# A three-stage kernel on one core: late states and their statistics in the head of the scan stage, and another order on VectorE in steps 7 to 11

## The chip, the core and the metric

The kernel runs on one core of a Trainium2 chip. The metric is the device time of one execution in microseconds. Times of single instructions come from one profiled execution of the program.

## What is computed

Input is a tensor of 4 batches, 1024 tokens and 256 channels, fp32. Three blocks with residuals follow each other: a coupled feed-forward, a selective scan (Mamba), and the same feed-forward again.

```python
x = x + 0.5 * ffn(layernorm(x))
x = x + mamba(layernorm(x))
x = x + 0.5 * ffn(layernorm(x))

def ffn(x):                       # 3 cycles over all tokens
    gf = global_net(x.mean(axis=1, keepdims=True))
    out = x
    for _ in range(3):
        tf = coupling_net(out)    # 256 -> 256 -> 128 -> 64 -> 1: gelu, gelu, gelu, sigmoid
        c = 0.1 + adaptive_range * (0.7 * gf + 0.3 * tf - 0.5) * 2.0
        out = out + c * twist(out)            # twist swaps and negates quarters of the channels
    return out

def mamba(resid):                 # 512 inner channels, 16 states, 4 taps
    xn = rmsnorm(resid) * norm_w
    skip, x = xn @ skip_w.T, xn @ in_w.T
    x = silu(conv4(x) + conv_b)
    delta = softplus(x @ wd1.T @ wd2.T + wd2_b)
    B, C, A = x @ wB.T, x @ wC.T, -exp(A_log)
    h[t] = exp(delta[t] * A) * h[t-1] + delta[t] * x[t] * B[t]     # per channel and state
    y[t] = sum_n h[t] * C[t] + W_D * x[t]
    return resid + (y * silu(skip)) @ out_w.T
```

## The kernel before

Three programs run one after the other, with a barrier between them: `ffn` ("f1"), `mamba`, and `ffn` ("f2"). The residual `x_tok` stays in SBUF as 32 tiles of 128 tokens by 256 channels, eight for each batch. Every engine runs a list of instructions in order; semaphores alone tie the lists together.

**The feed-forward.** There are 12 steps, one for each batch and cycle, in the order of `ORDER`: batches 0 and 1 alternate through their three cycles (steps 0 to 5), then batches 2 and 3 (steps 6 to 11). A step is a ring: gelu on ScalarE (L529), matmul (L412), gelu (L535), matmul (L424), gelu (L542), matmul (L435), tanh (L561), and on VectorE `update` (L245, L258, L260), whose result the same batch's next step reads two steps later. Since twist is linear, the kernel keeps the two products `a` and `b` of the first weight matrix instead of the state; `turn_by` (L268) and `turn_off` (L277) turn `b` after a batch's first cycle. `update` of a batch's second cycle reads the turned `b`, and the tanh of the second cycle overwrites the coupling that `turn_by` reads (`act.wait_ge(part_ready, ...)` in `tanh4`). The state after three cycles is a combination of the normalised input `z_tok` and its twist with coefficients per token. `coefficients` computes them (14 instructions on 8 elements, L289 to L311), `add_straight` (L319) or, for batches 2 and 3, `finish` on ScalarE (L569) adds the straight part, and `add_across` (L331, L333) the twisted one, 16 instructions for a batch. `measure` (L340, L344) then takes mean and variance of the new `x_tok` for the next normalisation. VectorE's order around the change is its loop over `s`: for s = 7, `coefficients(1)`, `add_straight(1)`, `update(6)`, `add_across(1)`, `turn_by(6)`, `turn_off(6)`; for s = 8, `coupling_base(3)`, `update(7)`, `turn_by(7)`; for s = 9, `update(8)`, `turn_off(7)`; then `update(9)` and, in f1, the two `measure`.

**The scan.** Eight segments of 512 tokens, each of 32 units K: 16 states times two pairs of channel tiles. Per unit, ScalarE writes the decays exp(delta A) into one of two PSUM banks (`decay`, L916), GpSimd the input term `u` into a ring of four (`drive`, L1030), VectorE runs two scans of 512 (L1113), and either VectorE (L1125) or, for 6 states of 16, GpSimd (`weigh`, L1042) multiplies with C. TensorE adds up. Between the units stands the preparation of the next segment by the places in `AT` and `PLACES`: turned tiles (L952), `acc` (L972), the taps of the convolution on VectorE (`convolve`, L1148, with the three columns kept for the next segment in `spill`, L1155 to L1164), silu (L977), projections, softplus over 2048 elements (L988), `take_in` on GpSimd (L1051, two products of delta and x). Segment 0 is prepared before the first scan, with nothing beside it. Ahead of that stand mean and deviation of all 32 tiles in one chain between ScalarE (L894, L896) and VectorE (L1083 to L1096).

## Time and profile before

| | |
|---|---|
| median of 3 runs | 1346.56 us (1346.34 to 1346.61) |
| profiled execution | 1345.62 us, span 1343.8 us |
| VectorE (DVE) | 87% of the span busy |
| GpSimd (POOL) | 65% |
| ScalarE (ACT) | 58% |
| TensorE (PE) | 79%, mean granted clock 0.943 |
| f1, up to its last instruction | 0 to 207.3 us |
| scan stage | 207.6 to about 1158 us |
| f2 | about 1158 us to the end |

Busy shares are means over the whole span, while the stages have different limits. In the rows, f_ stands for a tile of a feed-forward, m_ for one of the scan stage; a line "x8" joins eight like instructions in a row, from the start of the first to the end of the last, which overlap a little. A bracket tells how long the engine stood idle ahead of the instruction and whose end released it.

### The profile page before, as it was taken

How to read it: one execution, taken by the hardware profiler on the slowest of the kernel's cores; microseconds unless marked ns; L12 is line 12 of the kernel's file. 1: busy time of each engine (PE TensorE's matmuls, PEld its weight loads, DVE VectorE, ACT ScalarE, POOL GpSimd, SP SyncE). 2: the span in 40 equal slices, each digit the busy share in tenths (PEclk: the TensorE clock that was granted, in tenths of full speed). 3: DMA queues.
4: the chain of work that ended last, by engine and by line, in shares of the span. 5: the costliest groups of instructions: out<-in, count | busy, mean ns of one | idle time of the engine just before them, and what ended most of it. 6: DMA issues, size and time to landing. Idle time of an engine off the chain costs nothing. (4 is left out here: it accounts for less than half of the span.)

```text
span 1343.8 us, 10915 instructions
## 1 busy us (share of the span) xinstructions
PE 1065.7 (79%) x2688; PEld 459.1 (34%) x2688; DVE 1171.8 (87%) x1764; ACT 774.9 (58%) x1315; POOL 871.6 (65%) x390
## 2 busy tenths in 40 slices
PE   3999644679779889878888988987897867799964
PEld 2434212233233334324334333432432422444411
DVE  3755985599999999999999999999999999576595
ACT  2656465767645656745656674565674434266555
POOL 0000000899989999998999999899999999000000
PEclk9999887889998899999989999999998888899987
DMA  6000000544444444354353443445445443000003
GB/s 204 1 1 1 1 1 2 165 139 151 158 129 162 149 157 156 123 174 144 128 187 116 169 147 139 154 125 188 137 147 170 144 156 109 0 1 1 1 0 126
DMA packets 48000, 146.56 MB, mean 109 GB/s; under 512 B 5504, under 2 KB 14336, under 8 KB 47936
## 3 DMA queue, kind: packets, MB, share of 16 engines
q1 hardware_dynamic: 47440, 145.03, 32.6%
q10 hardware_dynamic: 496, 0.82, 0.2%
q8 instruction: 22, 0.36, 0.1%
q14 instruction: 42, 0.34, 0.1%
HBM read 141.05 MB, written 4.72 MB: 108 GB/s over the span
## 5 line engine op out<-in xcount | busy, mean ns | idle before, releaser
L1030 POOL TENSOR_TENSOR m_u<-m_dx,m_brow 128x1024 f32<-128x1024 f32 x256 | 599.4, 2380 | 1.0 <-DVE m_a_bank L1113 0.9
L916 ACT ACTIVATE m_a_bank<-m_delta,m_negA 128x512 f32<-128x512 f32 x512 | 335.0, 683 | 172.9 <-DVE m_hc L1125 133.4
L1259 PE MATMUL m_y_bank<-m_hc,ident 128*128 128x512 f32 x640 | 327.8, 638 | 102.3 <-DVE m_hc L1125 102.2
L1042 POOL TENSOR_TENSOR m_hc_pool<-m_hid,m_crow 128x1024 f32<-128x1024 f32 x96 | 228.5, 2380 | 28.7 <-DVE m_hid L1113 28.4
L1259 PEld LDWEIGHTS m_y_bank<-m_hc,ident 128*128 128x128 f32 x640 | 119.0, 199 | 289.6 <-DVE m_hc L1125 169.8
L1125 DVE TENSOR_TENSOR m_hc<-m_a_bank,m_crow 128x512 f32<-128x512 f32 x320 | 203.2, 678 | 0.0
L1113 DVE TENSOR_TENSOR_SCAN m_a_bank<-m_a_bank,m_carry,m_u 128x512 f32<-128x512 f32 x160 | 196.5, 1276 | 1.1 <-ACT m_a_bank L916 0.8
L1051 POOL TENSOR_TENSOR m_dx<-m_delta,m_x 128x1024 f32<-128x1024 f32 x16 | 38.1, 2385 | 240.1 <-ACT m_delta L988 240.1
L1259 PE MATMUL m_y_bank<-m_hc_pool,ident 128*128 128x512 f32 x384 | 187.8, 613 | 7.1 <-POOL m_hc_pool L1042 7.1
L1113 DVE TENSOR_TENSOR_SCAN m_a_bank<-m_a_bank,m_u 128x512 f32<-128x512 f32 x160 | 186.7, 1213 | 7.0 <-ACT m_a_bank L916 3.5
L1113 DVE TENSOR_TENSOR_SCAN m_hid<-m_a_bank,m_u 128x512 f32<-128x512 f32 x96 | 111.9, 1208 | 19.4 <-ACT m_a_bank L916 19.1
L1222 PE MATMUL m_w_bank<-m_xn,w 128*128 128x512 f32 x240 | 115.1, 608 | 3.7 <-DVE m_dx L1148 2.6
L1113 DVE TENSOR_TENSOR_SCAN m_hid<-m_a_bank,m_carry,m_u 128x512 f32<-128x512 f32 x96 | 117.8, 1270 | 0.0
L1259 PEld LDWEIGHTS m_y_bank<-m_hc_pool,ident 128*128 128x128 f32 x384 | 75.0, 198 | 105.7 <-issue 87.9
L412 PE MATMUL f_pair<-f_h,w 128*128 128x512 f32 x192 | 94.7, 624 | 6.1 <-ACT f_h L529 6.1
L928 ACT ACTIVATE m_carry<-m_a_bank 128x2 f32<-128x2 f32 x80 | 13.5, 169 | 109.5 <-DVE m_hc L1125 109.4
L529 ACT ACTIVATE f_h<-f_a,w 128x512 f32<-128x512 f32 x96 | 63.6, 713 | 10.8 <-DVE f_a L260 10.8
L1247 PE MATMUL m_y_bank<-m_x,m_diag_d 128*128 128x512 f32 x64 | 43.2, 811 | 33.4 <-DVE m_gate L1135 33.4
L1222 PEld LDWEIGHTS m_w_bank<-m_xn,w 128*128 128x128 f32 x240 | 45.8, 194 | 65.5 <-issue 53.9
L1236 PE MATMUL m_w_bank<-w,m_gate 128*128 128x256 f32 x256 | 59.1, 384 | 9.6 <-DVE m_dx L1148 8.1
L461 PE MATMUL f_pair<-f_z,w 128*128 128x512 f32 x128 | 65.4, 592 | 0.0
L1148 DVE SCALAR_TENSOR_TENSOR m_dx<-m_w_bank,m_conv,m_dx 128x511 f32<-128x511 f32 (+2 forms) x84 | 62.3, 741 | 1.1
(135 smaller groups left out, 1232.4 us busy)
## 6 DMA issues: line engine op xcount, KB each, us to landing
m_brow<-bc_rows SPq DMA_DIRECT2D x128, 512.0 KB, 4.9
m_crow<-bc_rows SPq DMA_DIRECT2D x128, 512.0 KB, 4.0
x_tok<-x_in SPq DMA_DIRECT2D x4, 1024.0 KB, 8.8
out<-x_tok SPq DMA_DIRECT2D x3, 1024.0 KB, 6.4
w<-w_in SPq DMA_DIRECT2D x1, 1024.0 KB, 12.4
out<-x_tok SPq DMA_DIRECT2D x4, 256.0 KB, 2.1
w<-w_in SPq DMA_DIRECT2D x1, 750.0 KB, 10.4
w<-w_in ACTq DMA_DIRECT2D x1, 512.0 KB, 6.0
```

The lines of the kernel that those rows point to most:

```text
L412: last = nc.tensor.matmul(pair[2][:, h, :], w(w256, W256, "w2", k), h1[:, k, half(h)], start=k == 0, stop=k == KD - 1)
L461: last = nc.tensor.matmul(out[:, m, :], second, z[:, b % 2, 1, half(n)], start=False, stop=True)
L529: nc.scalar.activation(h1[:, m, half(h)], source, ACT.Gelu, bias=w128[:, o:o + 1]).then_inc(h1_ready, 1)
L916: nc.scalar.activation(a_bank[K % 2][:, j, :], delta[:, i % 2, c, :], ACT.Exp, scale=negA[:, c, n:n + 1]).then_inc(S["a"], 1)
L1030: nc.gpsimd.tensor_tensor(u[:, K % U_RING, :, :], dx[:, i % 2, 2 * q:2 * q + 2, :], brow[:, K // 2 % ROW_RING, K % 2, :].unsqueeze(1).to_b ...
L1042: nc.gpsimd.tensor_tensor(hc_pool[:, before % POOL_RING, :, :], hid[:, before % POOL_RING, :, :], crow[:, K // 2 % ROW_RING, K % 2, :].uns ...
L1113: nc.vector.tensor_tensor_scan(hid[:, pool_before(K) % POOL_RING, j, :] if by_pool(K) else a, a, u[:, K % U_RING, j, :], 0.0 if i % 2 == 0 ...
L1125: nc.vector.tensor_tensor(hc[:, before % HC_RING, j, :], a_bank[K % 2][:, j, :], crow[:, K // 2 % ROW_RING, K % 2, :], ALU.mult).then_inc( ...
L1148: nc.vector.scalar_tensor_tensor(a[:, s:], b[:, 0:BANK - s], conv[:, c, k:k + 1], a[:, s:], ALU.mult, ALU.add)\
L1222: op = nc.tensor.matmul(b, w256[:, part, o:o + P], xn[:, (p if kind == "in" else i) % 2, part, :], start=part == 0, stop=part == KD - 1)
L1236: op = nc.tensor.matmul(b[:, part * DIM:(part + 1) * DIM], gate[:, d, at:at + P], col("out", d, DIM), start=d == 0, stop=d == KE - 1)
L1259: op = nc.tensor.matmul(y_bank[:, j, :], ident[:, :], source[:, before % ring, j, :], start=False, stop=K % PASS == PASS - 1)
```

## The change

The last states of batches 2 and 3 are no longer added and measured in f1. f1 leaves behind their coefficients (`coef`) and their normalised input (`late`, memory that the scan stage uses as its ring `u`), and the scan stage takes this over. The straight part of batch 2 goes from ScalarE to VectorE (`late_straight` there). Square roots and norms are taken in two halves: tiles 0 to 15 at once, 16 to 31 within segment 0 (`deviation` at units 4 and 8 on ScalarE, `norms` after units 5 and 10 on VectorE). ScalarE's instructions ahead of the first scan are written out in one list, `prologue`; the turned tiles of segment 1 are made there too, the standardising of `x_tok` for segments 0 and 1 comes in units 1, 3, 6 and 7. Softplus is split into two halves in all segments, and in segment 0 the second `take_in` of GpSimd moves to unit 3. VectorE keeps the spill columns of segment 0 after all taps, then adds and measures the late batches. In `ffn`, `coefficients` no longer contains the shifts that only batches 2 and 3 need, and the order of steps 7 to 11 is another, in f1 and f2 alike.

```diff
+def late_tile(mem, at):
+    return mem["late"][:, :, :, :].rearrange("p a b (c d) -> p (a b c) d", d=DIM)[:, at - 2 * BT, :]
...
-        z_tok = sb("z_tok", [P, TILES, DIM])
+        z_tok = sb("z_tok", [P, 2 * BT, DIM])
...
-                nc.vector.tensor_tensor(at(3), at(7), rstd[:, ts], ALU.mult).then_inc(coef_ready, 1)
-                dve.wait_ge(coef_ready, 2 * b + 1)
+                nc.vector.tensor_scalar(at(9), at(5), -0.5, None, ALU.mult).then_inc(coef_ready, 1)
+                dve.wait_ge(coef_ready, b + 1)
+            def shifts(b):
+                ts, n = slice(b * BT, (b + 1) * BT), b - len(ALONE) + 1
+                at = lambda j: coef[:, b % 2, j, :]
+                nc.vector.tensor_tensor(at(3), at(7), rstd[:, ts], ALU.mult).then_inc(shift_part, 1)
+                dve.wait_ge(shift_part, n)
                 nc.vector.tensor_scalar(at(10), at(3), 1.0, None, ALU.add)
                 nc.vector.scalar_tensor_tensor(at(11), at(3), -1.0, moments[:, ts, 0], ALU.mult, ALU.mult)\
-                    .then_inc(coef_ready, 1)
-                dve.wait_ge(coef_ready, 2 * b + 2)
+                    .then_inc(shift_ready, 1)
...
-                if s in (6, 7):
-                    add_across(s - 6)
-                if cycle(s - 1) == 0:
+                if s == 6:
+                    add_across(0)
+                if s == 8:
+                    turn_off(6)
+                if s in (1, 2, 7):
                     turn_by(s - 1)
-                    if s < 8:
-                        turn_off(s - 1)
+                if s in (1, 2):
+                    turn_off(s - 1)
                 if s == 9:
+                    turn_by(7)
                     turn_off(7)
                 if s == 2:
                     sum_up(2)
                 if s == 5:
                     coupling_base(2)
                     sum_up(3)
-                if s in (10, 11) and measure_next:
-                    measure(s - 10)
+                if s == 10:
+                    add_across(1)
+                if s == 11 and leave_late:
+                    measure(0)
+                    measure(1)
             coefficients(2)
-            add_across(2)
+            shifts(2)
+            if not leave_late:
+                add_across(2)
             coefficients(3)
-            if measure_next:
-                measure(2)
-            add_across(3)
-            if measure_next:
-                measure(3)
+            shifts(3)
+            if not leave_late:
+                add_across(3)
...
+            def norms(h, part):
+                ts = slice(h * (TILES // 2), (h + 1) * (TILES // 2))
+                root, square = roots[:, h, 0, :], roots[:, h, 1, :]
+                if part == 0:
+                    dve.wait_ge(S["root"], 2 * h + 1)
+                    nc.vector.reciprocal(rstd[:, ts], root).then_inc(S["rstd"], 1)
+                    dve.wait_ge(S["rstd"], 6 * h + 1)
+                    nc.vector.tensor_tensor(square, rstd[:, ts], rstd[:, ts], ALU.mult).then_inc(S["square"], 1)
+                    dve.wait_ge(S["square"], 2 * h + 1)
+                    nc.vector.tensor_tensor(square, square, moments[:, ts, 1], ALU.mult).then_inc(S["square"], 1)
+                    return
+                dve.wait_ge(S["root"], 2 * h + 2)
+                nc.vector.reciprocal(rrms[:, ts], root).then_inc(S["rstd"], 1)
+                dve.wait_ge(S["rstd"], 6 * h + 2)
+                nc.vector.scalar_tensor_tensor(shift[:, ts], moments[:, ts, 0], -1.0, rstd[:, ts], ALU.mult, ALU.mult)\
+                    .then_inc(S["rstd"], 1)
+                nc.vector.tensor_tensor(scale_n[:, ts], rstd[:, ts], rrms[:, ts], ALU.mult).then_inc(S["rstd"], 1)
+                nc.vector.tensor_scalar(scale_z[:, ts], rstd[:, ts], 1.0, None, ALU.add).then_inc(S["rstd"], 1)
+                dve.wait_ge(S["rstd"], 6 * h + 5)
+                nc.vector.tensor_tensor(shift_n[:, ts], shift[:, ts], rrms[:, ts], ALU.mult).then_inc(S["rstd"], 1)
+            def late_straight():
+                b = BATCH - 2
+                for t in range(BT):
+                    at = b * BT + t
+                    op = nc.vector.scalar_tensor_tensor(x_tok[:, at, :], late_tile(mem, at), coef[:, b % 2, 7, t:t + 1],
+                                                        x_tok[:, at, :], ALU.mult, ALU.add)
+                op.then_inc(S["late_by_dve"], 1)
+                dve.wait_ge(S["late_by_dve"], 1)
+            def late_across(b):
+                for t in range(BT):
+                    at, z = b * BT + t, late_tile(mem, b * BT + t)
+                    if b == BATCH - 1:
+                        dve.wait_ge(S["late_straight"], t + 1)
+                    nc.vector.scalar_tensor_tensor(x_tok[:, at, :P], z[:, P:], coef[:, b % 2, 8, t:t + 1],
+                                                   x_tok[:, at, :P], ALU.mult, ALU.add).then_inc(S["late_added"], 1)
+                    nc.vector.scalar_tensor_tensor(x_tok[:, at, P:], z[:, :P], coef[:, b % 2, 9, t:t + 1],
+                                                   x_tok[:, at, P:], ALU.mult, ALU.add).then_inc(S["late_added"], 1)
+            def late_measure():
+                first = (BATCH - 2) * BT
+                dve.wait_ge(S["late_added"], 4 * BT)
+                for t in range(2 * BT):
+                    op = nc.vector.bn_stats(late_stats[:, t, :], x_tok[:, first + t, :])
+                op.then_inc(S["late_stats"], 1)
+                dve.wait_ge(S["late_stats"], 1)
+                for t in range(2 * BT):
+                    op = nc.vector.bn_aggr(moments[:, first + t, :], late_stats[:, t, :])
+                op.then_inc(S["moments"], 1)
+            norms(0, 0)
+            norms(0, 1)
+            late_straight()
+            late_across(2)
...
+            def softplus(i, g):
+                p, cs = i + 1, slice(2 * g, 2 * g + 2)
+                act.wait_ge(S["step"], p * KE + 2 * g + 2)
+                nc.scalar.activation(delta[:, p % 2, cs], delta[:, p % 2, cs], ACT.Softplus).then_inc(S["delta"], 1)
...
+            def prologue():
+                act.wait_ge(S["rstd"], 6)
+                standardise(0, 0, xn_tok, scale_n, shift_n, "xn_tok")
+                standardise(0, 1, xn_tok, scale_n, shift_n, "xn_tok")
+                late_straight(range(4))
+                take_turned(-2, 0)
+                take_turned(-2, 1)
+                standardise(1, 0, xn_tok, scale_n, shift_n, "xn_tok")
+                standardise(1, 1, xn_tok, scale_n, shift_n, "xn_tok")
+                table_of(ACT.Silu)
+                accumulate(-1, 0)
+                late_straight(range(4, 6))
+                accumulate(-1, 1)
+                late_straight(range(6, 8))
+                accumulate(-1, 2)
+                accumulate(-1, 3)
+                silu(-1, 0)
+                silu(-1, 1)
+                take_turned(-1, 0)
+                silu(-1, 2)
+                take_turned(-1, 1)
+                silu(-1, 3)
+                project(-1)
+                table_of(ACT.Softplus)
+                step_size(-1, 0)
+                step_size(-1, 1)
+                softplus(-1, 0)
+                step_size(-1, 2)
+                step_size(-1, 3)
+                softplus(-1, 1)
+                rates()
...
+                for g, t in enumerate((1, 3, 6, 7)):
+                    if K == t:
+                        standardise(g // 2, g % 2, None, scale_z, shift, "z")
+                for n, t in ((2, 4), (3, 8)):
+                    if K == t:
+                        deviation(n)
...
+                if K == 0:
+                    pool.wait_ge(S["late_added"], 4 * BT)
...
+                    if (i, g) != (-1, 1):
+                        take_in(i + 1, g)
+                if K == 3:
+                    take_in(0, 1)
...
+                if K == AT["conv"][-1] - UNITS:
+                    for c in range(KE):
+                        keep_spill(-1, c, 1)
+                        keep_spill(-1, c, 2)
+                    late_across(BATCH - 1)
+                    late_measure()
+                if K in (5, 10):
+                    norms(1, K // 10)
```

## Rows read from the trace of the kernel before

**Rows 1.** The page, busy time of each engine, its share of the span and its instructions.

```profile
PE 1065.7 (79%) x2688; PEld 459.1 (34%) x2688; DVE 1171.8 (87%) x1764; ACT 774.9 (58%) x1315; POOL 871.6 (65%) x390
```

**Rows 2.** Windows, scan segment 0: window, length, busy us (instructions) per engine, PEclk, DMA.

```profile
250.00:363.00 113.00, 90.28 (x192) 35.42 (x191) 111.26 (x126) 74.83 (x147) 108.64 (x48) 0.95 0.45 150
```

**Rows 3.** Timeline, VectorE and ScalarE, steps 7 to 11: start, us, engine, line; idle before.

```profile
146.46 0.34 DVE L331 SCALAR_TENSOR_TENSOR x_tok<-f_z_tok,f_coef,x_tok 128x128 f32<-128x128 f32 x1
...
150.66 2.35 DVE L268 TENSOR_TENSOR f_part<-f_a,f_cpl 128x1024 f32<-128x1024 f32 x2
...
155.63 0.55 DVE L245 TENSOR_SCALAR f_cpl<-f_cpl,f_slope,f_base 128x512 f32<-128x512 f32 x1
...
161.59 2.35 DVE L268 TENSOR_TENSOR f_part<-f_a,f_cpl 128x1024 f32<-128x1024 f32 x2
...
148.10 1.26 ACT L561 ACTIVATE f_cpl<-f_pair,f_half_b 128x512 f32<-128x512 f32 x2 [1.21 <-PE f_pair L435]
...
158.73 1.33 ACT L529 ACTIVATE f_h<-f_a,w 128x512 f32<-128x512 f32 x2 [5.39 <-DVE f_a L260]
...
171.56 1.27 ACT L561 ACTIVATE f_cpl<-f_pair,f_half_b 128x512 f32<-128x512 f32 x2 [1.21 <-PE f_pair L435]
...
179.88 1.25 ACT L561 ACTIVATE f_stack<-f_pair,f_half_b 32x512 f32<-32x512 f32 x2 [1.21 <-PE f_pair L435]
...
1287.98 1.26 ACT L561 ACTIVATE f_cpl<-f_pair,f_half_b 128x512 f32<-128x512 f32 x2 [1.21 <-PE f_pair L435]
...
1311.52 1.27 ACT L561 ACTIVATE f_cpl<-f_pair,f_half_b 128x512 f32<-128x512 f32 x2 [1.21 <-PE f_pair L435]
```

**Rows 4.** Timeline, VectorE and TensorE at the end of the first feed-forward stage.

```profile
178.24 2.70 DVE L340 BATCH_NORM_STATS2 f_stats<-x_tok 128x6 f32<-128x256 f32 x8
...
185.04 0.24 DVE L289 COPY f_coef<-f_pair 128x8 f32<-128x8 f32 x2
...
186.92 0.16 DVE L311 SCALAR_TENSOR_TENSOR f_coef<-f_coef,moments 128x8 f32<-128x8 f32 x1
...
189.54 1.03 PE L468 MATMUL f_pair<-ident,f_stack 34*128 34x34 f32 x8 [1.38 <-issue]
...
206.66 0.64 DVE L344 BATCH_NORM_AGGREGATE moments<-f_stats 128x2 f32<-128x6 f32 x8
```

**Rows 5.** Timeline, all engines, head of the scan stage before its first scan.

```profile
209.23 0.35 DVE L1083 RECIPROCAL m_rstd<-m_tmp_u 128x32 f32<-128x32 f32 x1 [0.66 <-ACT m_tmp_u L894]
...
211.23 0.19 DVE L1096 TENSOR_TENSOR m_shift_n<-m_shift,m_rrms 128x32 f32<-128x32 f32 x1
...
212.28 2.08 ACT L938 ACTIVATE m_tmp_u<-x_tok,m_shift_n,m_scale_n 128x256 f32<-128x256 f32 x4
...
220.26 0.78 ACT L972 ACTIVATE m_dx<-m_a_bank,m_conv 128x512 f32<-128x512 f32 x1 [1.91 <-PE m_a_bank L1222]
...
229.35 0.27 DVE L1155 TENSOR_SCALAR m_spill<-m_a_bank,m_conv 128x3 f32<-128x3 f32 x1
...
230.57 0.74 DVE L1148 SCALAR_TENSOR_TENSOR m_dx<-m_a_bank,m_conv,m_dx 128x509 f32<-128x509 f32 x1
...
239.60 1.91 ACT L988 ACTIVATE m_delta<-m_delta 128x2048 f32<-128x2048 f32 x1
...
246.20 9.29 POOL L1030 TENSOR_TENSOR m_u<-m_dx,m_brow 128x1024 f32<-128x1024 f32 x4
...
249.65 2.34 DVE L1113 TENSOR_TENSOR_SCAN m_hid<-m_a_bank,m_u 128x512 f32<-128x512 f32 x2 [18.34 <-ACT m_a_bank L916]
```

**Rows 6.** Timeline, all engines, early units of scan segment 0.

```profile
257.56 2.29 DVE L1148 SCALAR_TENSOR_TENSOR m_dx<-m_w_bank,m_conv,m_dx 128x511 f32<-128x511 f32 x3
...
278.44 1.28 ACT L977 ACT_TABLE_LOAD   x1
...
283.39 1.30 ACT L916 ACTIVATE m_a_bank<-m_delta,m_negA 128x512 f32<-128x512 f32 x2
...
284.62 2.34 DVE L1113 TENSOR_TENSOR_SCAN m_a_bank<-m_a_bank,m_u 128x512 f32<-128x512 f32 x2
```

More of the change, by code:

```diff
@@ L631, in _ @@
             tanh4(STEPS - 1, 1)
-            finish(2)
-            finish(3)
+            if not leave_late:
+                finish(2)
+                finish(3)
         @block.sync
@@ L728, in mamba @@
     }
+    EARLY_TURN = ((4,), (5,))
     AT = {
@@ L786, in mamba @@
         here = [(at, kind, c, part) for kind in PLACES if exists(i, kind)
-                for c, ats in enumerate(PLACES[kind]) for part, at in enumerate(ats)]
+                for c, ats in enumerate(EARLY_TURN if (i, kind) == (-1, "turn") else PLACES[kind])
+                for part, at in enumerate(ats)]
         order = list(PLACES)
@@ L833, in mamba @@
         crow = sb("crow", [P, ROW_RING, 2, BANK])
-        u = sb("u", [P, U_RING, 2, BANK])
+        u = mem["late"]
+        expA = sb("expA", [P, KE, STATE])
+        roots = sb("roots", [P, 2, 2, TILES // 2])
         hid = sb("hid", [P, POOL_RING, 2, BANK])
@@ new lines, in take_turned, with accumulate @@
+            def take_turned(i, c):
+                b = work_there((i, "turn", c))
+                for d in range(KD):
+                    o = W128["norm"][0] + d
+                    op = nc.scalar.activation(xn[:, i % 2, d, c * 2 * P:(c + 1) * 2 * P],
+                                              b[:, d * 2 * P:(d + 1) * 2 * P], ACT.Copy, scale=w128[:, o:o + 1])
+                op.then_inc(S["xn"], 1)
+            def accumulate(i, c):
+                p = i + 1
+                ph = p % 2
+                b = work_there((i, "in", c))
+                if c == 0 and i > 0:
+                    act.wait_ge(S["u"], i * UNITS)
+                lo = 0
+                if ph == 1:
+                    lo = TAPS - 1
+                    act.wait_ge(S["spill"], p // 2 * KE + c + 1)
+                    for j in range(lo):
+                        nc.scalar.activation(acc[:, ph, c, j:j + 1], b[:, j:j + 1], ACT.Identity,
+                                             scale=conv[:, c, TAPS - 1:TAPS], bias=spill[:, c, j:j + 1])
+                nc.scalar.activation(acc[:, ph, c, lo:], b[:, lo:], ACT.Identity,
+                                     scale=conv[:, c, TAPS - 1:TAPS], bias=conv[:, c, TAPS:TAPS + 1])\
+                    .then_inc(S["acc"], 1)
@@ new lines, in silu, with project @@
+            def silu(i, c):
+                p = i + 1
+                act.wait_ge(S["conv"], p * KE + c + 1)
+                nc.scalar.activation(x[:, p % 2, c, :], acc[:, p % 2, c, :], ACT.Silu).then_inc(S["x"], 1)
+            def project(i):
+                p = i + 1
+                b = work_there((i, "xproj", 0))
+                if p > 0:
+                    act.wait_ge(S["bc_stored"], 16 * p)
+                nc.scalar.activation(proj[:, :], b[0:XROWS, :], ACT.Copy).then_inc(S["proj"], 1)
@@ L944, in turn @@
                 for g in due(k, "xn_tok"):
[L945 to L946 removed]
+                    if g == 0 and p == SEGS // 2:
+                        act.wait_ge(S["rstd"], 12)
                     standardise(p, g, xn_tok, scale_n, shift_n, "xn_tok")
                 for c in due(k, "xn"):
[L949 to L954 removed]
+                    take_turned(i, c)
                 for g in due(k, "z"):
@@ L1001, in take_out @@
                 nc.scalar.activation(th[:, c, :], b, ACT.Copy).then_inc(S["out_there"], 1)
-            for K in range(-2 * UNITS, TOTAL + UNITS):
+            prologue()
+            for K in range(TOTAL + UNITS):
                 i, k = K // UNITS, K % UNITS
@@ L1287, in build @@
             "moments": sb("moments", [P, TILES, 2]),
+            "late": sb("late", [P, 4, 2, BANK]),
+            "coef": sb("coef", [P, 2, 12, BT]),
         }
```

170 lines of the change are left out of this document (77 added, 93 removed).

## The prediction

> **What bounds the kernel now.** I read the page first. VectorE is busy 1171.8 of 1343.8 us [rows 1], but that is a mean over three stages, so I went to the windows. In one segment of the scan VectorE works 111.3 of 113.0 us and GpSimd 108.6 [rows 2]: VectorE sets the pace there, GpSimd stands 2.7 us behind it, and what is gained before the first scan is handed through to the end only if both start earlier. Then I read the timeline at the three places that the edits touch. The reader is to see three stretches in which VectorE is not paced by the scan. In steps 8 to 10 of each feed-forward stage ScalarE waits 5.39 us for `update` [rows 3]. After the last tanh of the first stage VectorE alone adds and measures until 207.30 (206.66 + 0.64) [rows 4]. From there to the first scan at 249.65 it is mostly idle, 18.34 us of it in one piece, while the chain ScalarE, TensorE, ScalarE prepares segment 0 [rows 5].
>
> The profiled execution took 1345.6 us, its span 1343.8; the median of the runs is 1346.6, 0.9 more. I sum against the profiled one and add 0.9 at the end.
>
> **Part 1, the order of steps 7 to 11.** Undisturbed, a tanh pair follows the last after 8.32 us (171.56 to 179.88). The two intervals from the pair of step 7 (148.10) to that of step 9 (171.56) should take 16.64 and take 23.46, so 6.8 are lost; in the second stage (1287.98 to 1311.52) 23.54, so 6.9 [rows 3]. The cause is VectorE's queue: between `update(6)` and `update(7)` stand 16 adds across (146.46 to 150.66, 4.2), `turn_by` and `turn_off` of step 6 and `coupling_base` (150.66 to 155.63, 5.0) [rows 3]. The new order puts only `turn_by(6)` (2.3) and the base (0.4) there. So `update(7)` starts at 149.2, after the tanh of 148.10 whose first half ends by 148.8. An update of two halves lasts 5.96 (155.63 to 161.59) [rows 3], its first half 2.98; that half is there at 152.2, and ScalarE wants it at 153.3 (158.73 − 5.39) [rows 3]: the 5.39 go. What is late next: `update(7)` ends at 155.2, `turn_off(6)` at 157.4, `update(8)` at 163.4 and `turn_by(7)` at 165.7. The second tanh of step 9 overwrites what `turn_by(7)` reads; it would start at 165.3 and starts 0.45 late. Then `turn_off(7)` holds `update(9)` until 167.9; its first half is there at 171.0, ScalarE wants it at 170.3: 0.7 more. Both pass on, since gelu, matmul and tanh make one ring. Second stage: 23.54 − 16.64 − 1.15 = **5.75 saved**. Its moved adds of batch 1 run at 1313.8 to 1318.0, before the coefficients of batch 2 at about 1319, and the store of batch 1, now behind them, lies under 20 us of other work.
>
> **Part 2, the end of the first stage.** Its last tanh ends at 183.8 and the transposes that take the coefficients over (1.35 later there, 189.54 start) end at 184.9. But VectorE decides: `update(9)` ends at 173.9, the adds of batch 1 (4.2) at 178.1, the two `measure` (6.8, 178.24 to 185.04) at 184.9, two sets of coefficients with their shifts (2.05 each, 185.04 to 187.08) at 189.2 [rows 4]. The adds and statistics of batches 2 and 3 are gone from here. 207.3 − 189.2 = **18.1 saved**.
>
> **Part 3, from there to the first scan.** Barrier, deviations and norms took 4.1 (207.30 to 211.42) [rows 5], so they end at 193.3. ScalarE starts 0.86 sooner after them, since the rates moved behind (212.28 against 211.42), and puts four straight adds of batch 3 in front of the turned tiles, at 0.52 each (2.08 for 4) 2.0 in all. From 211.42 to the first `acc` at 220.26 it was 8.84 [rows 5], so that starts at 193.3 + 8.84 − 0.86 + 2.0 = 203.3. VectorE's own adds of batch 2 (8 of 0.48, overlapped, 3.3, and 4.2) end at 200.8, hidden under this. The Silu table load (1.28, [rows 6]) lies under TensorE's first matmuls, 3.9 long. From here all is VectorE's: `acc` 0.78, four channel tiles of taps at 2.29 [rows 6] = 9.2, twelve small spill instructions, taken at 0.23 with their hand-overs from the 0.27 of the longest [rows 5] = 2.8, adds across of batch 3 4.2, statistics of 16 tiles 6.7. That is 227.0. The others are there by then: before, the softplus ended 10.2 after the last tap (231.31 to 241.51) [rows 5]; from 213.3 that makes 223.5, plus 0.2 for the split, 1.8 for table and rates and 0.7 for the first decay, less 1.3 for a table load moved under TensorE's work: 224.9. GpSimd now needs one product instead of two before its first `u`: the first softplus half is there near 220.0 (222.4 less its second half and two step sizes, 2.4), so that `u` starts near 222.4 and is written at 224.7 (products of 2.32, 9.29 for 4 [rows 5]). So the first scan starts at 227.0 instead of 249.65: with part 2 **22.7 saved**, 4.6 of it here. GpSimd's `u` starts 24 earlier and has one 2.3 product more to do at unit 3, so it keeps its lead and the gain is handed through.
>
> **Part 4, what comes back in segment 0.** VectorE is full there, so its extra work counts whole: the norms of batches 2 and 3 cost 1.8, as the same instructions did (209.23 to 211.42 is 2.2, with one square root on ScalarE between them, taken at 0.4) [rows 5]. ScalarE gets four pairs of standardised tiles, 1.0 each, and two Sqrt, each with table loads. In unit 4 it has room. In unit 8 it has not: the decay of unit 9 was half there at 284.05, the scan took it at 284.62 [rows 6]; a Sqrt of 0.3 and one load of 1.28 more give a wait of **1.0**. The split softplus adds 0.23 per segment (from 1.91 for 2048 elements [rows 5] and 0.65 for 512 [rows 6]) where the scan has 0.16 to spare: I take **0.5** in all, between 0 and 2. One price no row shows: in the scan every VectorE instruction has an operand in PSUM, but five of the norms' and the 16 adds across have both in SBUF while GpSimd runs. Nothing excludes 0; the other bound, by the nearest row, is a wait for one GpSimd product, 2.32 (9.29 for 4), each [rows 5]: 11.6 for five, and 2.3 for the adds, since only one product can run beside them before `u` waits for them. I take half a product for each of the two norm groups, **2.4**: VectorE comes upon a running product at random, and one wait lets the group through.
>
> The Trainium skill has a rule on just this (SBUF — State Buffer, Who interferes with whom): a VectorE instruction with two SBUF inputs and a GpSimd one that reads SBUF take turns, each blocked for the whole of the other. No run here shows it. By it the sum would go to the upper bound, rival A.
>
> Rows 6 show the Silu load at 1.28 us with no idle ahead of it. The Trainium skill (ScalarE: Activation LUTs, What ACT_TABLE_LOAD costs) puts 1.38 us of draining beside each load; by that the stall at unit 8 would be 2.4 and the time 1.4 longer. The trace has no room for it.
>
> **Sum.** 22.7 + 5.75 − 1.8 − 1.0 − 0.5 − 2.4 = 22.75 saved. 1345.6 − 22.75 = 1322.9, and at the median 1323.8 us. Under 0.2% (2.7 us) no run of this kernel can tell a change.
>
> **Rivals.**
> A. Each of the norms' five two-SBUF instructions waits for a whole product, and the adds across for one. For it: GpSimd works 108.6 of 113.0 us, so there is nearly always one running, and semaphores between them let the next begin. Against: the ring of four `u` makes GpSimd wait in the early units. 13.9 instead of 2.4: 1335.3.
> B. The new order brings nothing: `turn_by(7)`, `turn_off(7)` and the tanh that waits for them only move the wait. For it: 1.15 of that is in my own sum. Against: 1.0 of slack at `update(7)`. Then 5.75 go, and the first stage ends 3.5 later, with coefficients at 190.6 + 2.1: 1333.1.
> C. Slower: the second softplus half pushes ScalarE behind the ring of two decay banks in every segment. It decides from 2.9 us per segment (22.75 / 8). At one whole lost unit, 3.5 for 113/32, it costs 28: 1351.8. For it: only 0.16 of slack at that unit; against: the added instruction is 0.23.
> D. Less is given back: no port wait, the stall of unit 8 absorbed by small waits for GpSimd later, steps at full clock: 1317 to 1320.
> E. Nothing is handed through, since GpSimd sets the pace: excluded as far as I see, its `u` starts earlier too; within 0.2%.
>
> **How the numbers follow.** Forecast 0.60, with its own range of 1319.5 (2.4, 1.0 and some waits gone) to 1328 (twice the port waits, 2 for the softplus). A 0.13, B 0.10, C 0.04, D 0.06, E 0.02, and 0.05 for a mixture between forecast and B. The range for 8 in 10 is 1318 to 1334: forecast, B, the mixture, half of D. Faster 0.94, same 0.02, slower 0.04.
>
> **What would show it.** The tanh pairs of steps 7 and 9 16.7 apart, and the step after 9.5 long; VectorE's last instruction of the first stage at 189; first scan at 227, right behind the last statistics aggregate and not behind a decay; the scan of unit 9 with about 1 us of waiting; norms in units 5 and 10 of 0.2 us each, or of up to 2.5 if A holds; second stage 5.75 shorter. The prediction falls if the first scan waits for ScalarE or GpSimd, if the segments grow beyond 113 and 114, or if the step order gives no more than B says.

## The result, and the profile after

The changed kernel takes 1325.99 us (median of 4, 1325.21 to 1328.22) against 1346.45 (median of 4, 1345.24 to 1346.61) for the kernel before: ratio 0.9853, 95% interval 0.9836 to 0.9870. It is 20.5 us faster. The prediction said 1323.8 us within 1318 to 1334.

The profiled execution of the changed kernel took 1325.21 us, its span 1323.4. Cut at four instructions of VectorE that both kernels have, the two spans differ like this:

| us | before | after | difference | predicted |
|---|---|---|---|---|
| start to first scan | 249.65 | 224.78 | −24.87 | −22.65 |
| segment 0, first scan to the first scan with a carry | 109.75 | 119.66 | +9.91 | +5.2 to +5.7 |
| segments 1 to 7, to the first of the 16 statistics behind them | 789.45 | 789.71 | +0.26 | up to +0.5 |
| last stage | 194.95 | 189.25 | −5.70 | −5.75 |

First the page, busy time, share and instructions as in [rows 1]; then the window over segment 0, with the columns of [rows 2].

```profile
PE 1061.0 (80%) x2688; PEld 456.6 (35%) x2688; DVE 1184.1 (89%) x1768; ACT 774.8 (59%) x1321; POOL 872.6 (66%) x390
```

```profile
226.50:339.50 113.00, 84.01 (x168) 32.95 (x168) 110.92 (x123) 76.92 (x148) 100.55 (x44) 0.87 0.41 134
```

VectorE is as full in this window as before (110.9 of 113.0 us), but GpSimd does only 100.6 us of work in it where it did 108.6 [rows 2], and the window, of the same length, no longer holds the whole segment. An instruction that is held counts as busy, so VectorE looks busy while part of its time moves nothing forward. The granted clock is lower too (0.87 for 0.95). That is not what lengthened the segment: in experiment 3 the segment is short again, and the clock over it is 0.89.

The timeline of ScalarE and VectorE over steps 7 to 11 answers to [rows 3], with the last coefficient of the first stage and the head's last aggregate and first scan [rows 4, 5].

```profile
147.50 1.27 ACT L581 ACTIVATE f_cpl<-f_pair,f_half_b 128x512 f32<-128x512 f32 x2 [1.21 <-PE f_pair L455]
155.83 1.27 ACT L581 ACTIVATE f_cpl<-f_pair,f_half_b 128x512 f32<-128x512 f32 x2 [1.21 <-PE f_pair L455]
164.15 0.69 ACT L581 ACTIVATE f_cpl<-f_pair,f_half_b 128x512 f32<-128x512 f32 x1 [1.21 <-PE f_pair L455]
165.22 0.69 ACT L581 ACTIVATE f_cpl<-f_pair,f_half_b 128x512 f32<-128x512 f32 x1 [0.38 <-DVE f_part L279]
...
170.39 1.33 ACT L549 ACTIVATE f_h<-f_a,w 128x512 f32<-128x512 f32 x2 [0.50 <-DVE f_a L271]
173.51 1.25 ACT L581 ACTIVATE f_stack<-f_pair,f_half_b 32x512 f32<-32x512 f32 x2 [1.21 <-PE f_pair L455]
...
188.08 0.16 DVE L326 SCALAR_TENSOR_TENSOR coef<-coef,moments 128x8 f32<-128x8 f32 x1
...
201.51 0.78 ACT L1019 ACTIVATE m_dx<-m_a_bank,m_conv 128x512 f32<-128x512 f32 x1 [0.39 <-PE m_a_bank L1405]
...
218.34 5.32 DVE L1258 BATCH_NORM_STATS2 m_hc<-x_tok 128x6 f32<-128x256 f32 x16
...
224.78 2.30 DVE L1285 TENSOR_TENSOR_SCAN m_hid<-m_a_bank,late 128x512 f32<-128x512 f32 x2
```

The pairs of steps 7 and 9 stand 16.65 us apart (147.50 to 164.15). The next interval is 9.36 long (to 173.51), stretched by 0.38 for `turn_by(7)` and 0.50 for `update(9)`, the two places the prediction named. The first scan has no bracket: it follows VectorE's own statistics, and nothing else is late.

Where the time comes back is seen in VectorE's and GpSimd's timelines at the two places of the late norms.

```profile
248.40 0.24 DVE L1216 RECIPROCAL m_rstd<-m_roots 128x16 f32<-128x16 f32 x1
248.68 4.35 DVE L1218 TENSOR_TENSOR m_roots<-m_rstd 128x16 f32<-128x16 f32 x1
253.06 0.17 DVE L1220 TENSOR_TENSOR m_roots<-m_roots,moments 128x16 f32<-128x16 f32 x1
...
265.65 2.34 DVE L1285 TENSOR_TENSOR_SCAN m_a_bank<-m_a_bank,late 128x512 f32<-128x512 f32 x2 [1.10 <-ACT m_a_bank L957]
...
271.59 2.28 DVE L1225 SCALAR_TENSOR_TENSOR m_shift<-moments,m_rstd 128x16 f32<-128x16 f32 x1
273.79 0.16 DVE L1227 TENSOR_TENSOR m_scale_n<-m_rstd,m_rrms 128x16 f32<-128x16 f32 x1
273.88 2.32 DVE L1228 TENSOR_SCALAR m_scale_z<-m_rstd 128x16 f32<-128x16 f32 x1
276.23 0.17 DVE L1230 TENSOR_TENSOR m_shift_n<-m_shift,m_rrms 128x16 f32<-128x16 f32 x1
...
248.33 2.37 POOL L1167 TENSOR_TENSOR m_hc_pool<-m_hid,m_crow 128x1024 f32<-128x1024 f32 x1
250.63 2.36 POOL L1155 TENSOR_TENSOR late<-m_dx,m_brow 128x1024 f32<-128x1024 f32 x1
255.63 2.36 POOL L1155 TENSOR_TENSOR late<-m_dx,m_brow 128x1024 f32<-128x1024 f32 x1 [2.64 <-DVE m_a_bank L1285]
...
271.49 2.35 POOL L1167 TENSOR_TENSOR m_hc_pool<-m_hid,m_crow 128x1024 f32<-128x1024 f32 x1 [0.99 <-DVE m_hid L1285]
273.80 2.37 POOL L1155 TENSOR_TENSOR late<-m_dx,m_brow 128x1024 f32<-128x1024 f32 x1
```

Such an instruction on 16 elements lasts 0.16 to 0.17 us when nothing holds it. Three of six were held: one for 4.35, until two products of GpSimd had ended (at 252.99), and two for 2.28 and 2.32, each until the running product ended (273.84 and 276.17). The two groups take 4.75 and 5.00 us, 9.75 together (248.40 to 253.15, 271.33 to 276.33), of which 3 × 0.16 taken from 4.35 + 2.28 + 2.32 leaves 8.5 of waiting. And behind each group GpSimd stands 2.6 us for a scan that VectorE has not yet made (2.64 and 2.58, the second at 278.75).

### The profile page after: what moved, and what is told of

Its sections match the earlier page's. It is cut to its first block and busy times, and to the rows that moved or that the text cites. A ratio compares the mean times of both kernels' runs of the same rounds, so it can differ in the third digit from the quotient of the medians.

```text
span 1323.4 us, 10922 instructions
## 1 busy us (share of the span) xinstructions
PE 1061.0 (80%) x2688; PEld 456.6 (35%) x2688; DVE 1184.1 (89%) x1768; ACT 774.8 (59%) x1321; POOL 872.6 (66%) x390
## 5 line engine op out<-in xcount | busy, mean ns | idle before, releaser
L1155 POOL TENSOR_TENSOR late<-m_dx,m_brow 128x1024 f32<-128x1024 f32 x256 | 597.7, 2363 | 6.7 <-DVE m_a_bank L1285 6.5
L1442 PE MATMUL m_y_bank<-m_hc,ident 128*128 128x512 f32 x640 | 332.4, 645 | 116.1 <-DVE m_hc L1297 115.4
L1285 DVE TENSOR_TENSOR_SCAN m_a_bank<-m_a_bank,m_carry,late 128x512 f32<-128x512 f32 x160 | 196.4, 1274 | 1.1 <-ACT m_a_bank L957 0.8
L1285 DVE TENSOR_TENSOR_SCAN m_a_bank<-m_a_bank,late 128x512 f32<-128x512 f32 x160 | 186.7, 1212 | 7.0 <-ACT m_a_bank L957 3.7
L1285 DVE TENSOR_TENSOR_SCAN m_hid<-m_a_bank,m_carry,late 128x512 f32<-128x512 f32 x96 | 117.7, 1269 | 0.0
L1285 DVE TENSOR_TENSOR_SCAN m_hid<-m_a_bank,late 128x512 f32<-128x512 f32 x96 | 111.8, 1206 | 1.4 <-ACT m_a_bank L957 1.4
## 6 DMA issues: line engine op xcount, KB each, us to landing
w<-w_in SPq DMA_DIRECT2D x1, 1024.0 KB, 11.6
```

What stands on the lines that cost most here:

```text
L1155: nc.gpsimd.tensor_tensor(u[:, K % U_RING, :, :], dx[:, i % 2, 2 * q:2 * q + 2, :], brow[:, K // 2 % ROW_RING, K % 2, :].unsqueeze(1).to_b ...
L1285: nc.vector.tensor_tensor_scan(hid[:, pool_before(K) % POOL_RING, j, :] if by_pool(K) else a, a, u[:, K % U_RING, j, :], 0.0 if i % 2 == 0 ...
L1442: op = nc.tensor.matmul(y_bank[:, j, :], ident[:, :], source[:, before % ring, j, :], start=False, stop=K % PASS == PASS - 1)
```

## The experiments

**1 and 2. The order of steps 7 to 11 by itself.** Once the changed kernel with the old order (its diff below, shortened), once the kernel before with the new order and nothing else of the change, the same lines the other way round.

```diff
-                if s == 6:
-                    add_across(0)
-                if s == 8:
-                    turn_off(6)
-                if s in (1, 2, 7):
+                if s in (6, 7):
+                    add_across(s - 6)
+                if cycle(s - 1) == 0:
                     turn_by(s - 1)
...
-                if s == 10:
-                    add_across(1)
...
```

> The changed kernel with the order of steps 7 to 11 as it was before, in both feed-forward stages. Theory (the order is worth 5.7 us in the last stage and, since VectorE alone decides the end of the first, some 3.5 there): 9 us slower than the changed kernel, about 1335, ratio to before 0.9918; the pairs of tanh of steps 7 and 9 are 23.5 apart again instead of 16.6. Rival (the order only moves a wait, the gain is all of the late states): within 1.5 us of the changed kernel, about 1326.

> The kernel before with the new order of steps 7 to 11 alone, nothing else of the change. Theory: 5.7 us in the last stage and about 3.2 in the first, where VectorE's queue from update(9) on (30.2 us of adds, coefficients and statistics) ends at 204.1 instead of 207.3: about 1337.5, ratio 0.9934. Rival (the two parts are worth something only together): under 2 us, 1344.5 or more.

The first took 1336.13 us (1335.78 to 1336.67), ratio 0.9924 [0.9911, 0.9938]; the second 1337.78 (1336.05 to 1339.22), ratio 0.9936 [0.9922, 0.9949]. So the order is worth 10.1 us on top of the rest and 8.4 us without it (the kernel before took 1346.16 in that series). ScalarE's timeline of the first:

```profile
148.54 1.26 ACT L575 ACTIVATE f_cpl<-f_pair,f_half_b 128x512 f32<-128x512 f32 x2 [1.21 <-PE f_pair L449]
...
159.17 1.34 ACT L543 ACTIVATE f_h<-f_a,w 128x512 f32<-128x512 f32 x2 [5.38 <-DVE f_a L271]
...
172.52 1.27 ACT L575 ACTIVATE f_cpl<-f_pair,f_half_b 128x512 f32<-128x512 f32 x2 [1.21 <-PE f_pair L449]
```

The 5.38 of waiting and the 24.0 us from pair to pair are back. Its first scan starts 5.4 later (230.18) and its last stage is 6.3 longer (195.57) than the changed kernel's; segment 0 is the same (119.60). That is more than the 3.5 and 5.7 expected; why the first stage loses 5.4 was not followed up. In the second the last stage has its 5.9 (189.07 against 194.95) but the first scan gains only 3.0 (246.68): its first stage still ends with all the adds and statistics, at 204.49 instead of 207.30. Rival B is out.

**3. The late norms on GpSimd.** In the changed kernel the late norms' six instructions that are no reciprocal go to GpSimd's queue, behind its units 9 and 14 (as seven, since it gets the negated product in two steps). The two reciprocals stay.

```diff
+            def late_norms(part):
...
+                nc.gpsimd.tensor_tensor(scale_n[:, ts], rstd[:, ts], rrms[:, ts], ALU.mult).then_inc(S["rstd"], 1)
+                nc.gpsimd.tensor_scalar(scale_z[:, ts], rstd[:, ts], 1.0, None, ALU.add).then_inc(S["rstd"], 1)
...
+                if K in (9, 14):
+                    late_norms((9, 14).index(K))
```

> The changed kernel with the five two-input instructions of the late norms and the one that adds 1 moved from VectorE to GpSimd, after its units 9 and 14; the two reciprocals stay on VectorE. Theory (VectorE waited 8 us there for GpSimd's running products): segment 0 shrinks from 119.7 to about 111, the kernel to about 1317.5, ratio 0.9785, and the reciprocals stay at 0.25 us each. Rival (segment 0 is long because ScalarE and GpSimd are short of lead after the earlier start, and the long instructions only show it): the wait comes back ahead of a scan, under 2 us gained, 1324 or more.

It took 1315.52 us (1315.33 to 1319.93), ratio 0.9778 [0.9764, 0.9792]. Three of the five times lie at 1315.3 to 1315.5, some 10.5 us below the changed kernel, and two at 1319.7 and 1319.9, some 6 below it. The trace belongs to the 1319.93; in it segment 0 is 112.4 long instead of 119.7. VectorE and then GpSimd where the 4.35 and the second group had been:

```profile
249.13 0.24 DVE L1236 RECIPROCAL m_rstd<-m_roots 128x16 f32<-128x16 f32 x1
249.29 2.28 DVE L1309 TENSOR_TENSOR_SCAN m_a_bank<-m_a_bank,late 128x512 f32<-128x512 f32 x2
...
272.18 0.24 POOL L1189 TENSOR_TENSOR m_shift<-moments,m_rstd 128x16 f32<-128x16 f32 x1
272.36 0.24 POOL L1190 TENSOR_TENSOR m_scale_n<-m_rstd,m_rrms 128x16 f32<-128x16 f32 x1
272.55 0.28 POOL L1191 TENSOR_SCALAR m_scale_z<-m_rstd 128x16 f32<-128x16 f32 x1
```

The reciprocal lasts 0.24 and the scan follows it at once; on GpSimd each costs 0.22 to 0.28. This tests the cause of the 9.75 us. All but 0.3 of them (two reciprocals, each 0.16 ahead of its scan) leave VectorE. The segment is shorter by less than these 9.4, by 7.3 in this trace and by 8.7 in a second one of the same kernel (number 10 below, 110.93 long), since VectorE then waits somewhat more ahead of its scans.

**4. The price of one such instruction, measured by itself.** One extra instruction on 16 elements after each scan unit of segments 2 and 3, four kinds in turn, into memory that nobody reads. They wait for no semaphore, so a long one is held by something else.

```diff
+                if 66 <= K < 98:
+                    out, a, b = probe[:, K - 66, :], rstd[:, 0:16], rrms[:, 0:16]
+                    if K % 4 == 0:
+                        nc.vector.reciprocal(out, a)
+                    elif K % 4 == 1:
+                        nc.vector.tensor_tensor(out, a, b, ALU.mult)
+                    elif K % 4 == 2:
+                        nc.vector.tensor_scalar(out, a, 1.0, None, ALU.add)
+                    else:
+                        nc.vector.tensor_scalar(out[:, 0:8], a[:, 0:16:2], 1.0, None, ALU.add)
```

> The changed kernel with one small VectorE instruction more on 16 elements in each of 32 units of the second and third segment, while GpSimd is busy: in turn a reciprocal, a product of two SBUF tiles, an addition of a constant on contiguous elements, and the same addition on 8 elements with stride 2. Their results are used by nothing. Theory (an instruction with two SBUF inputs, and one with one input that is read in the fast two-port way, wait for the running product of GpSimd): reciprocal 0.2 us always; product up to 2.4 and above; contiguous addition up to 2.4; the strided addition tells whether contiguity matters, 0.2 if it does. Rival (any small VectorE instruction can be held by GpSimd): the reciprocals are held as often as the others.

One run: 1348.1 us, 22 more than the changed kernel. The groups of this trace over the two segments, busy us and mean ns:

```profile
L1383 DVE TENSOR_SCALAR m_probe<-m_rstd 128x16 f32<-128x16 f32 x8 | 10.7, 1339 | 0.0
L1381 DVE TENSOR_TENSOR m_probe<-m_rstd,m_rrms 128x16 f32<-128x16 f32 x8 | 8.2, 1026 | 0.0
L1385 DVE TENSOR_SCALAR m_probe<-m_rstd 128x8 f32<-128x8 f32 x8 | 6.2, 769 | 0.0
L1379 DVE RECIPROCAL m_probe<-m_rstd 128x16 f32<-128x16 f32 x8 | 1.9, 232 | 0.0
```

And one moment of its timeline, VectorE and then GpSimd:

```profile
471.82 6.76 DVE L1383 TENSOR_SCALAR m_probe<-m_rstd 128x16 f32<-128x16 f32 x1
...
469.29 4.66 POOL L1156 TENSOR_TENSOR late<-m_dx,m_brow 128x1024 f32<-128x1024 f32 x2
473.92 2.33 POOL L1168 TENSOR_TENSOR m_hc_pool<-m_hid,m_crow 128x1024 f32<-128x1024 f32 x1
476.22 2.33 POOL L1156 TENSOR_TENSOR late<-m_dx,m_brow 128x1024 f32<-128x1024 f32 x1
```

The reciprocal is never held. The other 24 cost 25.1 us, 1.05 each against 0.14 to 0.16 unheld; 14 of them lasted more than 0.3. The 27 us of all 32 (about 5.5 of them their own work) more than account for the 22. The longest, 471.82 to 478.58, ends with the third product since (478.55): a held instruction does not always get in when the product that it met ends. The tensor_scalar with one SBUF input is held like the product of two, and eight elements at a stride of 2 do not free it.

**5. Halves in steps 9 and 10.** `turn_by(7)` between the halves of `update(8)`, and `turn_off(7)` and `update(9)` half by half.

```diff
...
+                if s == 9:
+                    update(8, 0)
+                    turn_by(7)
+                    update(8, 1)
+                elif s == 10:
+                    for h in range(HALVES):
+                        turn_off(7, (h,))
+                        update(9, h)
...
```

> The changed kernel with two edits in VectorE's order of the FFN stages: in step 9 turn_by(7) stands between the two halves of update(8), and in step 10 update(9, h) follows turn_off(7, h) half by half. My theory: in the last stage ScalarE's tanh in step 9 stands 0.38 us for VectorE's product and in step 10 0.50 us for update(9); both waits go, the last stage becomes some 0.9 us shorter, and since the first stage ends with VectorE's own work nothing is won there: 1325.1 us, ratio to the kernel before 0.984. Rival: the engines behind (the multiplications of the last batches on TensorE, the DMAs) end last in the last stage anyway, and the time stays 1326.0.

It took 1324.22 us (1323.81 to 1325.96), ratio 0.9837 [0.9824, 0.9851]: 1.8 below the changed kernel, within the spread of the two. The trace tells it better (ScalarE, last stage):

```profile
1290.20 1.26 ACT L586 ACTIVATE f_cpl<-f_pair,f_half_b 128x512 f32<-128x512 f32 x2 [1.21 <-PE f_pair L460]
...
1298.52 1.25 ACT L586 ACTIVATE f_stack<-f_pair,f_half_b 32x512 f32<-32x512 f32 x2 [1.21 <-PE f_pair L460]
```

8.32 between the pairs, with both waits gone. From the pair of step 7 to that of step 11 it is 33.29 us (1273.55 to 1306.84) against 34.31 (1273.42 to 1307.73): 1.02 won, and from there to the end both need 15.7. By the times alone the gain is not shown; by the trace it is.

**6. The second root three units later.** The second square root behind unit 11 instead of 8, the second group of norms after scan unit 13 instead of 10.

```diff
-                for n, t in ((2, 4), (3, 8)):
+                for n, t in ((2, 4), (3, 11)):
...
-                if K in (5, 10):
-                    norms(1, K // 10)
+                if K in (5, 13):
+                    norms(1, K // 13)
```

> The changed kernel with the second square root of the late norms behind unit 11's decay instead of unit 8's, and the second group of late norms on VectorE after scan unit 13 instead of 10. My theory: the stall of 1.10 us before the scan of unit 9 comes from the root and its table load standing between the decays of units 8 and 9; moved back, ScalarE has had three more units to run ahead, but the kernel before too stood 0.92 us at unit 13 at a like place, so the stall moves rather than goes: 1325.5 us, between 1324.9 and 1326.3. The small norms go on being held by GpSimd's products, as another place has products too. Rival: the stall goes for good (1324.9) or the norms fall into an idle gap of GpSimd, and then some 4 us go as well (1322).

It took 1324.81 us (1324.17 to 1325.16), ratio 0.9839 [0.9825, 0.9852]. VectorE and GpSimd:

```profile
276.59 2.35 DVE L1285 TENSOR_TENSOR_SCAN m_a_bank<-m_a_bank,late 128x512 f32<-128x512 f32 x2 [0.86 <-ACT m_a_bank L957]
...
280.90 1.03 DVE L1225 SCALAR_TENSOR_TENSOR m_shift<-moments,m_rstd 128x16 f32<-128x16 f32 x1
281.85 2.38 DVE L1227 TENSOR_TENSOR m_scale_n<-m_rstd,m_rrms 128x16 f32<-128x16 f32 x1
284.15 0.16 DVE L1228 TENSOR_SCALAR m_scale_z<-m_rstd 128x16 f32<-128x16 f32 x1
...
279.53 4.67 POOL L1155 TENSOR_TENSOR late<-m_dx,m_brow 128x1024 f32<-128x1024 f32 x2
```

The stall moves (1.10 at unit 9 becomes 0.86 later), as the theory had it. Segment 0 is 1.2 shorter (118.48), nearly all of it since the second group met the product at another moment: 3.8 us (280.62 to 284.44) instead of 5.0. It is now `m_shift` and `m_scale_n` that are held, and `m_scale_z` not: which one waits hangs on where in a product the group arrives.

**7. Softplus whole again in segments 1 to 7.**

```diff
+                if i >= 0:
+                    act.wait_ge(S["step"], (p + 1) * KE)
+                    nc.scalar.activation(delta[:, p % 2], delta[:, p % 2], ACT.Softplus).then_inc(S["delta"], 2)
+                    return
```

> The changed kernel with the softplus of a segment as one operation of 128x1024 again in segments 1 to 7, and in two halves only ahead of segment 0. My theory: ScalarE saves one fixed cost of some 0.09 us in each of seven segments (2.00 for the two halves against 1.91), and the scans wait for ScalarE in part only, so at most 0.6 us and likelier 0.3: 1325.7 us. Rival: the halves start earlier than the whole can and so hide part of themselves; then the whole is slower by up to the length of one half in every segment in which ScalarE is behind, 7 x 1 us, 1333.

It took 1327.34 us (1325.96 to 1327.49), ratio 0.9856 [0.9842, 0.9869]: no difference that can be told. Segments 1 to 7 took 789.46 against 789.71 in the two traces. So the split costs about 0.3 there, too little for the times to show, and rival C is out.

**8 to 11. Both gains together, and the norms once more.** Number 8 has the edits of 3 and 5. Number 9 is number 8 with the norms later (diff below); numbers 10 and 11 are numbers 3 and 8 once more, one execution and one trace each.

```diff
-                for n, t in ((2, 4), (3, 8)):
+                for n, t in ((2, 4), (3, 37)):
...
-                if K in (9, 14):
-                    late_norms((9, 14).index(K))
+                if K in (21, 45):
+                    late_norms((21, 45).index(K))
...
-                if K in (5, 10):
-                    norms(1, K // 10)
+                if K in (5, 40):
+                    norms(1, K // 40)
```

> The changed kernel with the halves order of the run on it and with the late norms with two inputs on GpSimd after its units 9 and 14. My theory: the two gains add, as they lie in different stages: 1315.5 - 0.9 = 1314.6 us, ratio 0.977. Rival: no more than the norms alone, 1315.5, if the last stage does not end with the chain through ScalarE's tanh.

> The kernel of the last run with the late norms set later: GpSimd's first two small products after its unit 21 and the other five after unit 45 (not 9 and 14), the second square root on ScalarE behind unit 37 (not 8), VectorE's second reciprocal after scan unit 40 (not 10). The norms are used first in the preparation of segment 4, so all of it is in time. My theory: in segment 0 the three engines are closest together; there the kernel of the last run stood 1.10 us before the scan of unit 9 for the root and 2.41 us before a later scan, where GpSimd's five small products (1.2 us) and ScalarE's wait for the projection (5.0 us) come together. With the norms in later segments the 1.10 goes and the 2.41 falls by up to 1.2: 2.3 us less than the run before, 1316.9 against its 1319.16, or 1312.8 where its shorter times (1315.0) are the rule. Rival: GpSimd and ScalarE are as full in the segments behind, the waits move with the work, and the time stays within 0.5 us.

> The kernel with the late norms on GpSimd once more, for a second trace of it: its five times lay at 1315.3 to 1315.5 (three) and 1319.7 to 1319.9 (two), and the trace belongs to a 1319.9. My theory: the 4.4 us come from the wait of 2.15 us before one scan of segment 0 and the wait for TensorE before a gate (4.1 in sum against 2.1), both set by how fast TensorE ran at the head of the stage; a 1315 would show neither. Rival: they come from the FFN stages.

> The kernel with the halves order and the late norms on GpSimd once more, for a second trace, with the same question as the run before this one: a time near 1315 would show in which stage the 4 us between its times lie; a time near 1319 adds nothing.

Number 8 took 1319.16 us (1314.96 to 1319.31), ratio 0.9788 [0.9775, 0.9801]; number 9 1316.48 (1315.72 to 1317.25), ratio 0.9777 [0.9764, 0.9791]; numbers 10 and 11 gave 1315.92 and 1315.82. The kernels of 3 and 8 have times near 1315.5 and near 1319.5, and two traces of each show the difference. For the kernel of number 3, a window over four us of segment 0 in the 1319.9 (first) and in the 1315.9 (second):

```profile
264.00:268.00 4.00, 2.69 (x3) 1.17 (x4) 4.00 (x7) 1.85 (x5) 3.00 (x3) 0.59 0.44 115
```

```profile
264.00:268.00 4.00, 3.23 (x8) 1.56 (x9) 4.00 (x6) 2.39 (x6) 3.00 (x2) 1.00 0.31 125
```

The same four matmuls that stand in it, in the same two:

```profile
265.31 3.38 PE L1466 MATMUL m_y_bank<-m_hc,ident 128*128 128x512 f32 x4 [2.64 <-DVE m_hc L1321]
```

```profile
264.77 1.98 PE L1466 MATMUL m_y_bank<-m_hc,ident 128*128 128x512 f32 x4 [2.63 <-DVE m_hc L1321]
```

And the wait of VectorE in segment 0 that differs most, in the same two:

```profile
275.41 2.35 DVE L1309 TENSOR_TENSOR_SCAN m_a_bank<-m_a_bank,late 128x512 f32<-128x512 f32 x2 [2.15 <-ACT m_a_bank L957]
```

```profile
273.48 2.35 DVE L1309 TENSOR_TENSOR_SCAN m_a_bank<-m_a_bank,late 128x512 f32<-128x512 f32 x2 [0.75 <-ACT m_a_bank L957]
```

TensorE's granted clock is 0.59 there in the one and 1.00 in the other, and the four matmuls take 1.40 us longer; ScalarE then stands 4.74 against 3.35 us for the projection of the next segment, with the decays queued behind it, and VectorE 2.15 against 0.75. At the last gate it is the same: clock 0.81 over the 18 us ahead of it against 1.00, and VectorE waits 4.07 against 2.08. With 0.54 in the head (first scan at 225.52 against 224.98) that makes nearly the 4.0 between the spans. For the kernel of number 8 it is 2.1 in the head (clock 0.78 from 200 to 226 against 0.96) and 1.6 in segment 0. That VectorE's own lateness covers such waits while the norms stand on it is likely, but not shown: the changed kernel's times, too, range over 3.0 us, and it has one trace. What makes the clock fall in one execution and not in the next stays open: TensorE had stood 2.64 and 2.63 us before that stretch in the two. Number 9 loses the stall of 1.10, as I had it, and segment 0 is down to 110.24 (number 8 has 112.57, number 11 110.94), but segments 1 to 7 grow from 789.4 to 790.8: the rival is nearer, the waits moved with the work. Its 1316.48 is close to the 1316.9 expected from number 8's 1319.16, but by luck; against number 11's 1315.82 nothing is won. None of the three kernels (3, 8 and 9) is shown to be the best; at their lower times all lie some 10 us below the changed kernel.

## Why the prediction was right, and where it was off

The sign, the places and most of the sizes held; one term, the price of the late norms, did not. Point by point:

- **Part 1** was right to the tenth: 5.70 for 5.75. The 0.45 and 0.7 that `turn_by(7)` and `update(9)` were to cost were 0.38 and 0.50 of waiting; the interval behind them was 9.34 long in the last stage, 1.02 over the undisturbed 8.32, and experiment 5 takes both away and wins these 1.02.
- **Part 2** said 18.1 and it was 19.1 (last instruction at 188.24); 0.6 of that had come already before step 7, whose tanh stood at 147.50 instead of 148.10. Another 0.2 is a slip of addition: the prediction's own terms (173.9 + 4.2 + 6.8 + 4.1) end at 189.0, not 189.2.
- **Part 3** said the first scan at 227.0, right behind the last aggregate; it was there, at 224.78. Of the 2.2, 1.0 are from part 2, 0.3 from barrier and norms, 0.5 from norms to `acc` (9.46 for 9.98), and 0.4 from there on (23.27 for 23.7).
- **Part 4** has the step that failed. The waiting of VectorE's small norms beside GpSimd was taken at 2.4 us, on the ground that "one wait lets the group through"; it was 8.5. Each instruction meets the products anew: the one behind a held one came through (0.16), and the next was held again, as GpSimd had started its next product 0.08 us before. And I counted only instructions with two SBUF inputs; `m_scale_z`, a tensor_scalar with one, took 2.32. Rival A (13.9, of which 11.6 for the norms) had the mechanism more nearly than the forecast, and its sign, norms of up to 2.5 us, came, while the forecast's 0.2 each did not. But by no means each instruction waits (three of six without the reciprocals), and one wait is not bounded by one product, as the 4.35 shows. The adds across, for which A put 2.3, cost nothing: they end at 218.3, where GpSimd's first product has just begun.
- The stall at unit 9 was 1.10 for 1.0. But a stall of 0.92 at unit 13 that the kernel before had is gone, so only 0.2 of it counts. The softplus split cost 0.3 or less for 0.5.

The errors partly cancel: 2.2 more gained ahead of the first scan, and 4.7 more given back in segment 0 (9.9 for 5.2 without the softplus; the waits of the norms are 6.1 over, their own work is 0.5 under the 1.8, and the vanished stall takes off 0.9), which leaves the time 2.2 above the forecast. That the time came so near is in part luck: with part 4 as it was and the rest as forecast it would have been near 1328.5. One of the prediction's signs of failing, "if the segments grow beyond 113 and 114", did not fit its own sum, which put segment 0 at 115; segments 1 to 7 stayed at 112.8 each, and segment 0 became 119.7.

The rule that I had set beside the rows (the Trainium skill, SBUF — State Buffer, Who interferes with whom) fits these traces better than my estimate. It says that whichever engine comes first blocks the other for the whole of its instruction, and it also names tensor_scalar as an operation that can take the shared ports, which I had passed over; the 2.32 of `m_scale_z` agrees with that, and the reciprocal, which it does not name, was not held. The other direction shows as well. GpSimd's first product starts beside VectorE's last add across, and it is longer the more the two overlap: 2.45 us at 0.23 of overlap (number 8), 2.54 at 0.31 (the changed kernel), 2.60 at 0.37 (number 11), where a like product takes 2.36 later on (232.14 in the changed kernel). This fits with the adds costing VectorE nothing: in the changed kernel the last of them was running first. What the rule does not say is that a waiting VectorE instruction can lose the next turn too, as the 4.35 and the 6.76 show. For a table load the traces decide against a drain of 1.38 us beside it (the Trainium skill, ScalarE: Activation LUTs, What ACT_TABLE_LOAD costs): the second Sqrt load stands at 258.29 right behind a decay that ends at 258.27, takes 1.28, and the root starts at 259.58.

## What to carry to other kernels

Before small VectorE instructions whose inputs all lie in SBUF (products of two tiles, tensor_scalar) are put into a stretch where GpSimd runs products without a pause, count one possible wait for each of them, and not one for the group. A wait is mostly up to one product of GpSimd, and sometimes longer; in the fourth run 14 of 24 waited. Where the order allows it, let GpSimd do the small work in its own queue. A stage that one engine fills to 98% takes each such wait at its full length, however short the instruction is. And a gain ahead of such a stage is handed through only if whatever was moved into it is free there: here 10 of 25 us came back.

## What the runs showed of the hardware that I had not expected

A small VectorE instruction was held over two products of GpSimd (4.35 us) and over most of three (6.76), while GpSimd's products ran on one behind the other. A reciprocal of 16 elements took 0.22 to 0.24 us in every case, four of the fourth run's eight (from 487.64, 503.93, 533.78 and 564.58) in the middle of a running product. The same program had TensorE at a granted clock of 0.59 in one execution and of 1.00 in another in the same four us (1.2 GHz in part of them, or 2.4 throughout), four like matmuls took 3.38 us in the one and 1.98 in the other, and three stretches of that kind make nearly all of the 4.0 us between the two spans. A product of GpSimd that met a running two-input add of VectorE was the longer the more the two overlapped (2.45 us at 0.23, 2.60 at 0.37).
